# The down products of the first expert layer as three bf16 products, with two added passes that split their rows

## The reference, cut to what matters

```python
comb = (one_hot(topk_idx, E) * topk_val[..., None]).sum(axis=-2)   # 2 of 8 experts for each row
for e in range(E):
    h = jnp.einsum('btd,hd->bth', x, W1[e]) + b1[e]                # 128 -> 512
    a, b = jnp.split(h, 2, axis=-1)
    g = a * jax.nn.sigmoid(b)                                      # 256 wide
    eo = jnp.einsum('bth,dh->btd', g, Wo) + bo                     # 256 -> 128: the down products
    out = out + eo * comb[..., e:e + 1]
```

## Time and profile before

| | us |
|---|---|
| median of 3 runs | 1036.5 (1034.56, 1036.5, 1045.42) |
| the profiled execution | 1037.47, of which the span of the core is 1035.6 |
| the stage changed, from 193 to 410 us of the span | 217 |

### The profile page before, as it was taken

How to read it: one execution, slowest core, us unless ns; L and a number is a source line. 1 busy time by engine, 2 the same in 40 slices (tenths; PEclk the granted TensorE clock), 3 DMA queues, 4 the chain that set the end, 5 groups by cost and what they waited for, 6 DMA issues and landing times.

```text
span 1035.6 us, 22555 instructions
## 1 busy us (share of the span) xinstructions
PE 754.5 (73%) x8774; PEld 588.0 (57%) x8780; DVE 663.7 (64%) x1182; ACT 624.8 (60%) x1187; POOL 446.3 (43%) x463
## 2 busy tenths in 40 slices
PE   3847667889989996078763777687878878788760
PEld 3535445778878886055541454455766666666540
DVE  7756445676666653786676545566686677677547
ACT  4364334777686654456541444575877778777665
POOL 4266554024534546100003666324546556556532
PEclk9976787999999999587885778789998899998775
DMA  9711111101111111700002422300111111110063
GB/s 313 270 41 48 52 57 52 32 23 47 43 38 45 45 48 37 188 1 1 1 2 64 161 78 69 81 11 24 40 33 37 29 40 37 38 32 27 17 161 104
DMA packets 62363, 63.87 MB, mean 62 GB/s; under 512 B 7378, under 2 KB 52322, under 8 KB 62132
## 3 DMA queue, kind: packets, MB, share of 16 engines
q1 hardware_dynamic: 53300, 43.99, 14.7%
q0 software_dynamic: 8960, 18.43, 5.5%
HBM read 31.84 MB, written 30.55 MB: 60 GB/s over the span
## 4 chain that ended last, share of the span: by engine, by line
PE 47%; DVE 22%; issue 12%; ACT 12%; another core or an unknown queue 4%; DMA 1%; POOL 1%; SPq 1%; DVEq 0%; ACTq 0%
PE bank L716 4%; PE bank L686 4%; PE bank L769 3%; PE bank L670 3%; ACT arena L1204 3%; PE bank L781 3%; DVE arena L1729 2%; DVE arena L1495 2%; PE bank L742 2%; PE bank L484 2%; PE bank L486 2%; PE bank L526 2%; PE bank L485 2%; ACT L864 2%
## 5 line engine op out<-in xcount | busy, mean ns | idle before, releaser
L1880 POOL DMA_INDIRECT ys<-arena x152 | 168.7, 1110 | 201.5 <-ACT arena L1133 66.7
L1861 POOL DMA_INDIRECT xs<-arena x128 | 130.3, 1018 | 74.3 <-issue 32.5
L1204 ACT ACTIVATE arena<-bank 128x512 f32<-128x512 f32 x192 | 98.8, 599 | 86.9 <-PE bank L769 58.2
L1729 DVE TENSOR_REDUCE arena<-bank 128x2 bf16<-128x512 f32 (+1 forms) x192 | 119.0, 683 | 49.2 <-PE bank L742 43.1
L656 PE MATMUL bank<-arena 128*128 128x128 bf16 x608 | 107.1, 221 | 10.0 <-issue 3.5
L658 PE MATMUL bank<-arena 128*128 128x128 bf16 x608 | 107.2, 220 | 0.0
L657 PE MATMUL bank<-arena 128*128 128x128 bf16 x608 | 107.2, 221 | 0.0
L864 ACT ACT_TABLE_LOAD x72 | 92.4, 1283 | 1.3
L1717 DVE SCALAR_TENSOR_TENSOR arena<-arena,bank 128x512 bf16<-128x512 bf16 x64 | 46.3, 746 | 70.9 <-ACT arena L1177 67.2
L656 PEld LDWEIGHTS bank<-arena 128*128 x608 | 60.4, 99 | 15.4 <-issue 9.0
L716 PE MATMUL bank<-arena 128*128 128x256 f32 x256 | 65.7, 403 | 0.8 <-issue 0.8
(11 more groups left out here) (229 smaller groups left out, 2048.0 us busy)
## 6 DMA issues: line engine op xcount, KB each, us to landing
xs<-arena SPq DMA_DIRECT2D x19, 516.0 KB, 9.1
arena<-xs SPq DMA_DIRECT2D x38, 258.0 KB
arena<-ys SPq DMA_DIRECT2D x32, 256.0 KB, 5.1
arena<-in_MF SPq DMA_DIRECT2D x8, 512.0 KB
ys<-arena POOLq DMA_INDIRECT x152
arena<-in_x SPq DMA_DIRECT2D x8, 256.0 KB, 5.6
arena<-in_W SPq DMA_DIRECT2D x8, 256.0 KB, 2.7
xs<-arena POOLq DMA_INDIRECT x128
```

The source lines that it names most:

```text
L1204: act(PT[kt_][:, i, gs[0]:gs[0] + len(gs), :], bank_of["s2", b, n, i][:, :].rearrange("p (g q) -> p g q", q=w), ACT.Exp, scale=8 ** -0.5). ...
L1729: red(negM[b % 2][:, u, 32 * i + gs[0]:32 * i + gs[0] + len(gs)], kv_, op=ALU.max, negate=True).then_inc(m_max.sem, 1)
L1861: eng.indirect_dma_start(xs[l][:, :], bass.IndirectOffsetOnAxis(ap=slot_i[l][:, m:m + 1], axis=0), xrow[:, t, :], None).then_inc(rows_move ...
L1880: eng.indirect_dma_start(ys[l][:, :], bass.IndirectOffsetOnAxis(ap=yid[g % 4][:, j:j + 1], axis=0), y[:, 128 * j:128 * j + 128], None).the ...
```

## The change

The hidden rows of each group and the weights `Wo` are split into a bf16 high part and a bf16 rest, and `down0` multiplies high by high, high by low and low by high.

```diff
+        Y1b = pos[0]
...
+        halves_w = (arena[:, Y1b:Y1b + 1024], sb(1024))
+        hs = [w.bitcast(BF16).rearrange("p (z c) -> p z c", z=2) for w in halves_w]
+        Wo0b = sb(512, BF16).rearrange("p (z c d) -> p z c d", z=2, c=2)
...
-        set_pool, set_dve = sig("set_pool", 14), sig("set_dve", 19)
+        set_pool, set_dve = sig("set_pool", 16), sig("set_dve", 19)
...
-        f0_tanh, f0_h = sig("f0_tanh", 2), sig("f0_h", 2)
+        f0_act, f0_h = sig("f0_act", 3), sig("f0_h", 3)
...
@@ down0, TensorE @@
-                        i = mm(k[:, 128 * j:128 * j + 128], hb[g % 2][:, 256 * j + 128 * c:256 * j + 128 * c + 128], Wo0[:, c, :],
-                               start=(c == 0), stop=(c == 1))
+                        o, hc = k[:, 128 * j:128 * j + 128], slice(256 * j + 128 * c, 256 * j + 128 * c + 128)
+                        mm(o, hs[g % 2][:, 0, hc], Wo0b[:, 0, c, :], start=(c == 0), stop=False)
+                        mm(o, hs[g % 2][:, 0, hc], Wo0b[:, 1, c, :], start=False, stop=False)
+                        i = mm(o, hs[g % 2][:, 1, hc], Wo0b[:, 0, c, :], start=False, stop=(c == 1))
...
@@ ScalarE @@
+            def hidden_hi(g):
+                eng.wait_ge(*f0_h.at(g, 1))
+                act(hs[g % 2][:, 0, :], hb[g % 2], ACT.Copy).then_inc(f0_act.sem, 1)
+
             def ffn0(g, part):
                 if part < 2 and g < 18:
                     gates0(g, part)
+                if part == 2 and g < 18:
+                    hidden_hi(g)
...
@@ VectorE @@
+            def hidden_lo(g):
+                eng.wait_ge(*f0_act.at(g, 2))
+                tt(hs[g % 2][:, 1, :], hb[g % 2], hs[g % 2][:, 0, :], ALU.subtract).then_inc(f0_h.sem, 1)
+
             def ffn0(g, part):
...
                 if part == 2 and g >= 1:
                     biased0(g - 1)
+                if part == 2 and g < 18:
+                    hidden_lo(g)
...
@@ set_later, GpSimd @@
+                eng.wait_ge(*set_pool.at(0, 11))
+                eng.tensor_copy(Wo0b[:, 0], Wo0).then_inc(set_pool.sem, 1)
+                eng.wait_ge(*set_pool.at(0, 12))
+                tt(Wo0b[:, 1], Wo0, Wo0b[:, 0], ALU.subtract).then_inc(set_pool.sem, 1)
```

More of the change, by code:

```diff
@@ L642, in expert_up @@
                     if l == 0:
-                        bank(("b", g, j // 2), f0_tanh.at(g, j // 2))
+                        bank(("b", g, j // 2), f0_act.at(g, j // 2))
                         bank(("a", g, j // 2), f0_h.at(g, j // 2))
@@ L1076, in gates0 @@
                     eng.wait_ge(*routed[0].at(0))
-                act(thb[p], bank_of["b", g, p][:, :], ACT.Tanh, scale=0.5).then_inc(f0_tanh.sem, 1)
+                act(thb[p], bank_of["b", g, p][:, :], ACT.Tanh, scale=0.5).then_inc(f0_act.sem, 1)
+            def hidden_hi(g):
+                eng.wait_ge(*f0_h.at(g, 1))
+                act(hs[g % 2][:, 0, :], hb[g % 2], ACT.Copy).then_inc(f0_act.sem, 1)
             def ffn0(g, part):
@@ L1583, in hidden0 @@
             def hidden0(g, p):
-                eng.wait_ge(*f0_tanh.at(g, p))
+                eng.wait_ge(*f0_act.at(g, p))
                 if p == 0 and g >= 2:
```

## The result

The changed kernel takes 1058.68 us (median of 4 runs: 1051.34, 1057.29, 1060.07, 1060.08), where the kernel before takes 1035.53 in the same session: a ratio of 1.0189, 95% interval 1.0108 to 1.0269. The profiled execution took 1060.08 with a span of 1058.1. The forecast was 1046, with a range up to 1052: the sign was right, the size was not. By the profiles the span grew by 22.5 us.

What follows compares the result with a forecast made beforehand. By shares TensorE bounds the stage, but VectorE's and ScalarE's queues were to delay it: 0.25 + 3.2 + 4.2 + 1.4 + 1.9 - 1.35 = +9.6 us on 1036.5, so 1046, range 1038 to 1052.

Steps and rivals of the forecast that it cites:

- +0.8 us a turn: Groups 1, 4, 7, 10: VectorE's subtraction ahead of `scaled` delays `project` and `turn` by 0.8 us, 3.2 in all.
- +1.9: Groups 13+14: late up products, then copy, subtraction and `lo` ahead of the states, cost 1.9 us.
- 3 x -0.45: Groups 15 to 17, without queries and keys: TensorE bounds them, so shorter down products win 0.45 us each, -1.35.
- free: End of group 17: down products' 2.2 us wait for copy and subtraction is covered by GpSimd's last stores; uncovered 1.8.
- Prices and the step of the products: Each group: subtraction 1.226 us, copy 1.080; 24 bf16 down products at 0.056 each, 1.35 instead of 1.79.
- The rival that the products aren't cheaper: Down products: 24 bf16 take 1.79 us like the f32 ones, total 1047.4, or 0.9 longer, some 1051; chance 0.05.
- +1.4 for each such pair: Groups 2+3, 5+6, 8+9: subtraction, then ScalarE's copy ahead of `hi`, make the next tanh late; 4.2 us in all.
- the 0.45 goes into the wait for the bank: Attention turns: the 0.45 us TensorE gains on down products is spent waiting for the bank that `scaled` frees.

Runs made afterwards that it cites:

- the idle slots: Changed kernel with copy and subtraction moved to early in the next turn, at its head or behind its tanh and `hidden0`: 985.95 us, 1.0029 of the kernel before.
- the forced collision: Changed kernel with GpSimd's first store in groups 3, 6, 9, 12 waiting for ScalarE's copy, so it runs beside the subtraction: 998.21 us, 1.0114 of the kernel before.

## Why the prediction was wrong in size and right in sign

The step that failed is the sum of the stage's terms, and with it the range. First, "+0.8 us a turn" in attention turns: TensorE's wait was right, what follows it was left out, and a subtraction costs 1.13 to 1.16. Second, the granted clock, for which there was no term: on the first chip it fell three times in the stage. Third, the end of the stage: "+1.9", "3 x -0.45" and "free" are +1.18 together instead of +0.55. On the second chip the measured sum is +10.9 for +9.6, on the first +15.8. The other 6.6 us of the first chip's profile lie outside the stage, where the forecast had nothing, and their cause stays open.

**Prices and the step of the products.** Right: 1.22, 1.06, 0.056 us. The last timeline of TensorE, for group 17 in the first of the second chip's profiles, shows the step (24 products, of which first and last):

```profile
385.43 0.22 PE L675 MATMUL bank<-arena 128*128 128x128 bf16 x1 [2.00 <-DVE arena L1617]
...
386.72 0.22 PE L677 MATMUL bank<-arena 128*128 128x128 bf16 x1
```

1.29 / 23 = 0.056. The rival that the products aren't cheaper is out. The Trainium skill's rule on the issue gap (TensorE: Matmul & The Clock Gate, Back-to-back issue gap; 81 ns) disagrees with this trace too.

**"+0.8 us a turn" in attention turns.** Right place and right wait, under-sized. With f32 products as with bf16 ones, TensorE is idle for 0.78 us ahead of `project` until the first `scaled` is done. The run with the subtraction alone, group 4:

```profile
232.81 0.71 PE L565 MATMUL bank<-arena 128*128 128x128 f32 x4 [0.78 <-DVE arena L1548]
```

What the forecast lacked stands behind that wait: `project` and `turn` take 0.71 and 0.54 us of the chain, where they took 0.45 each. 0.78 + 0.35 is the +1.13 of that turn. Why the products behind a wait take longer isn't shown.

The 0.45 us of the down products don't go into this wait but into one before it. In the changed kernel the queries and keys have to wait, here in the first chip's profile:

```profile
220.79 0.27 PE L488 MATMUL bank<-arena 128*128 128x256 bf16 x1 [0.43 <-DVE arena L1511]
```

They read what VectorE's `chunk_lo` (L1511) writes. With the down products 0.44 us shorter, TensorE reaches them early and waits right there, ahead of the bank of `project`. The same 0.43 us stand there in the run without the subtraction, where `project` doesn't wait and the turn of group 1 is as long as before.

**"+1.4 for each such pair", by ScalarE's copy.** The total was about right, in part by luck: some 0.3 us too little for what follows the wait, and 0.3 for the copy, which alone costs nothing here. A cycle of three groups (4, 5+6) was to cost 0.8 + 1.4 = 2.2; it costs 1.88 + 0.61 = 2.49 in the second chip's profile, and 2.37 where the pair took 22.88. It is two subtractions, one in each attention turn, that make 2.3 (subtraction alone: 2.35). What the copy does, as the traces read, is to take the gain. In the changed kernel the pair is 0.7 us shorter than with f32 products (22.88 against 23.60), since here the shorter down products do bring TensorE forward. The next turn is 0.7 us longer (18.49 against 17.78), since its tanh stands at the end of a run of ScalarE that begins with the copy. The run without the subtraction shows the same give and take with the other cost gone: -0.63, +0.60. And where the copy of group 6 stands behind the tanh of group 7, in the idle slots, groups 5+6 and 7 together are 0.16 shorter than before; 0.33 is paid back in group 7 even there, so the copy isn't all of it. **That the products win nothing in the attention turns was right; "the 0.45 goes into the wait for the bank" is replaced by the wait for `chunk_lo` and by this.**

**"Free", at the end of group 17.** Wrong, though by little. The forecast read from the timeline that GpSimd issues its last eight stores one after another and needs group 17 only for the fifth. But `store(0, 16, 1)`, the third and fourth of them, waits in the code for the down products of group 17. Their result was early enough before, and it no longer is (GpSimd, the changed kernel on the second chip):

```profile
385.22 0.96 POOL L1902 DMA_INDIRECT ys<-arena  x1 [0.30 <-issue]
387.22 0.96 POOL L1902 DMA_INDIRECT ys<-arena  x1 [1.04 <-PE bank L677]
```

The gap is 1.04 instead of 0.30, so 0.74 us, and the tail's first store of group 16 is 0.45 later: together the measured +1.18. In the first chip's profile the third of them doesn't wait: there the first takes 1.71 us beside the last subtraction, and GpSimd is late itself. With f32 products and a subtraction this wait is 1.69 us, and group 17's products behind it take 3.35 us by the timeline, where the kernel before has 1.95 (mean clock from 387 to 395 us: 0.79), which is part of that kernel's long tail:

```profile
389.77 3.35 PE L675 MATMUL bank<-arena 128*128 128x128 f32 x16 [1.71 <-DVE arena L1613]
```

**"+1.9" and "3 x -0.45".** On the second chip the bias of group 14 is 0.3 us late by the last scan, where the forecast had +1.9 by then, and from there to the first fetch it is +0.9 instead of -1.35. The forecast took the passes of groups 15 to 17 as hidden. They aren't. The bias of group 16 comes 41.98 us behind the last scan in the kernel before, 42.76 with the copy alone, 42.40 in the changed kernel, and 45.44 with both passes and f32 products. The last has a fall of the clock in it, and the changed kernel's profile with such a fall has 43.11. So like against like the products win 2.3 us there, 0.45 for each of five groups, and the passes take about 2.7.

**What the sum had no term for: the granted clock.** The forecast took 1.00 for the whole stage. On the first chip it fell behind 2.13 us without work in the turn of group 4. TensorE and the windows of the first chip's profile:

```profile
256.16 0.59 PE L544 MATMUL bank<-arena 64*32 64x64 f32 x32 [2.13 <-DVE arena L1562]
```

```profile
257.00:258.00 1.00, 1.00 (x25) 0.83 (x16) 0.87 (x2) 0.59 (x2) 0.99 (x2) 0.50 0.25 78
```

The keys turned take 1.92 us at 0.50 and the turn 19.41; the like turn of the second chip at 1.00 takes 18.51. Turns with a fall are 0.6 to 1.0 us longer than their likes without. It comes and goes: behind 1.96 us of waiting the clock stayed at 1.00 in one run, behind 1.44 and 0.56 us it fell in another. The first chip's profile has three such falls, in the turns of groups 4 and 10 (256 to 260 and 341 to 346 us) and in the tail (382 to 387), each behind a wait of 2.1 us: about 2 to 2.5 of the stage's 5 us more, if the one in the tail costs what the others do. Another 1.1 are pieces of 0.1 to 0.3 in the other turns with the clock at 1.00. The rest is in the tail; it wasn't broken down.

**What stays open.** On the first chip 5.6 us more were lost ahead of the scan in group 0's turn and 1.0 behind the stage, where all but two passes on GpSimd and some places in the SBUF are as before; that those aren't the cause wasn't tried there. On the second chip that scan comes at 160.09 and 160.48 us with the change and at 160.32 and 161.42 without. The four runs of the changed kernel in the first session differ by 8.7 us, those of the kernel before by 11.4. No run came from the first chip again, so whether that chip makes this change dearer or the session was unlucky isn't settled. The second chip's +10 would lie within the forecast's range (up to 1052), which had nothing in it for the rest.

## What to carry to other kernels

A pass can cost nothing or its whole duration by where it stands in its engine's queue: look for what is behind it, and put it where that waits for something else anyway; the same 36 passes cost 10 us in one order and, placed ahead of waits, let the kernel win 0.4%. A shorter product on the engine that "bounds" wins only until the next wait, so name that wait before the gain is counted, here one for `chunk_lo` in the same turn and a tanh one turn later. And behind a wait count more than the wait: here 0.35 us beside 0.78. Last, read the program, not only the timeline, for who waits: a wait that was satisfied early (the third of the last eight stores, the queries and keys for `chunk_lo`) leaves no idle time in the trace of before, and is the first to show once things move.

## What the runs showed of the hardware

GpSimd's indirect stores slow down beside VectorE's subtraction. First chip, groups 2 and 3, timelines of GpSimd and VectorE:

```profile
249.49 1.94 POOL L1902 DMA_INDIRECT ys<-arena  x1 [1.51 <-DVE arena L1612]
...
252.72 0.86 POOL L1928 TENSOR_TENSOR arena<-arena 128x256 f32<-128x256 f32 x1
```

```profile
249.35 1.23 DVE L1617 TENSOR_TENSOR arena<-arena 128x1024 bf16<-128x1024 f32 x1
...
252.91 2.81 DVE L1507 TENSOR_TENSOR_SCAN arena<-arena 128x1024 f32<-128x1024 bf16 x1
```

The store takes 1.94 us instead of 0.96, and the scan 2.81 instead of 2.29 beside the multiply. Over the kernel the stores' mean goes from 1110 to 1207 ns:

```profile
L1902 POOL DMA_INDIRECT ys<-arena x152 | 183.5, 1207 | 199.7 <-ACT arena L1145 64.3
```

The Trainium skill has the rule (SBUF — State Buffer, Who interferes with whom): a VectorE instruction with two inputs in SBUF contends with a GpSimd instruction that reads SBUF, and the one that comes second is blocked. The trace agrees, if the store, which reads its row numbers from the SBUF, counts as such an instruction: the store at 216.76 of the forced collision ends at 218.50, 0.86 us after the subtraction's end at 217.64, nearly its own duration. The forecast had no price for this; in the turns it turned out to need none, as the forced collision showed.

The second surprise is the size of what a change doesn't touch: the kernel before takes 1035 us in one session and 984 in the others, with the turns up to group 10 equal to 0.01 us. 29 of the 54 us between the two spans lie ahead of these turns, 22 behind the stage.
